# Gelu expert layer: GpSimd prepares the second spline expert's weights, and that expert's store and the fifth expert's load move ahead of the routed tiles

## The reference, cut to what matters

```python
hs = gelu(einsum('td,nfd->ntf', t, sw1) + sb1)           # 2 shared experts, F = 512
shared = einsum('ntf,ndf->td', hs, sw2) + sb2.sum(0)
probs = softmax(t @ gate_w.T + gate_b)                    # 8 routed experts
top_v, top_i = top_k(probs, 2)
hr = gelu(einsum('td,efd->etf', t, rw1) + rb1)
routed = einsum('etd,te->td', einsum('etf,edf->etd', hr, rw2) + rb2, cw)
out = shared + routed
```

```python
spline = einsum('nic,oic->no', b_splines(x), spline_w * scaler[..., None])   # three such layers per expert, 8 experts
```

## Time and profile before

| | us |
|---|---|
| median of 3 runs | 922.3 |
| the three runs | 946.85, 922.3, 920.98 |
| profiled execution | 915.97 |
| its span | 914.2 |
| TensorE busy | 787.8 |
| VectorE busy | 619.0 |
| ScalarE busy | 559.5 |
| GpSimd busy | 287.9 |

### The profile page before, as it was taken

One profiled execution on the slowest core, in us unless ns is written; L12 is line 12 of the kernel. 1 busy time (PEld: TensorE's weight loads), 2 busy tenths in 40 slices (PEclk: granted clock), 3 DMA queues, 4 the chain that ended last, 5 costly groups with the idle time before them and its releaser, 6 DMA issues.

```text
span 914.2 us, 21932 instructions
## 1 busy us (share of the span) xinstructions
PE 787.8 (86%) x7434; PEld 739.0 (81%) x7434; DVE 619.0 (68%) x1347; ACT 559.5 (61%) x1339; POOL 287.9 (31%) x320
## 2 busy tenths in 40 slices
PE   4987999688950896549999999999999999999992
PEld 3865699677640684449999999999999999999992
DVE  3898869262565496554777777777787777777752
ACT  4872537454400794234888877778777777787650
POOL 1770056240565384011132222332232222222111
PEclk9995999798985597558999999999999999999997
DMA  9602668998892000262357362244544334420000
GB/s 350 277 4 66 277 180 318 358 373 316 334 419 84 1 3 23 77 244 85 110 166 269 88 221 87 63 124 154 166 165 164 122 108 146 136 61 11 8 7 6
DMA packets 53603, 141.08 MB, mean 154 GB/s; under 512 B 6459, under 2 KB 29381, under 8 KB 46373
## 3 DMA queue, kind: packets, MB, share of 16 engines
q1 hardware_dynamic: 40996, 110.47, 33.0%
q10 hardware_dynamic: 3408, 20.06, 5.7%
q0 software_dynamic: 9136, 9.77, 5.6%
HBM read 106.65 MB, written 33.62 MB: 153 GB/s over the span
## 4 chain that ended last, share of the span: by engine, by line
PE 53%; DVE 3%; ACT 1%; DMA 1%; issue 1%; POOL 0%; DVEq 0%; POOLq 0%; ACTq 0%
PE kan_ps_h L1607 33%; PE kan_ps_y L1621 17%; DMA kan_slot_x<-normed_dram,slots 1%; PE kan_ps_slots L1288 1%; PE kan_ps_slots L1296 1%; PE kan_ps_lists L1274 1%; PE kan_ps_x L1595 0%; PE kan_ps_h L1270 0%; DMA out<-kan_y_sb,kan_slots_y 0%; ACT kan_xt L1654 0%; DVE kan_hf L1756 0%; DVE kan_hfar L1752 0%; DVE kan_hnear L1753 0%; ACT kan_hnear L1668 0%; DVE kan_hf L1760 0%
## 5 line engine op out<-in xcount | busy, mean ns | idle before, releaser
L1607 PE MATMUL kan_ps_h<-kan_xf,kan_w 128*128 128x128 f32 x2496 | 306.3, 276 | 0.0
L1607 PEld LDWEIGHTS kan_ps_h<-kan_xf,kan_w 128*128 128x128 f32 x2496 | 293.3, 193 | 0.0
L1621 PE MATMUL kan_ps_y<-kan_w,kan_hf 128*128 128x128 f32 x1248 | 154.2, 277 | 8.3 <-DVE kan_hf L1760 8.3
L1621 PEld LDWEIGHTS kan_ps_y<-kan_w,kan_hf 128*128 128x128 f32 x1248 | 147.5, 194 | 8.8 <-issue 8.8
L1837 POOL DMA_INDIRECT out<-kan_y_sb,kan_slots_y x39 | 63.5, 1628 | 240.3 <-ACT kan_y_sb L1705 240.3
L1752 DVE TENSOR_TENSOR kan_hfar<-kan_ht,kan_hfar 128x1024 f32<-128x1024 f32 x39 | 48.1, 1233 | 84.4 <-ACT kan_hnear L1668 84.4
L1654 ACT ACTIVATE kan_ht<-kan_hu,kan_biases 128x256 f32<-128x256 f32 x156 | 66.2, 496 | 13.6 <-DVE kan_hu L1779 13.6
L1009 POOL DMA_INDIRECT f_slot_x<-normed_dram,f_tokens x39 | 42.7, 1096 | 96.7 <-DVE f_rows L1136 52.9
L554 DVE TENSOR_TENSOR sw_raw<-sw_raw,sw_scal 128x512 f32<-128x512 f32 x56 | 34.6, 691 | 50.3 <-DMA sw_scal<-in_scalers 50.3
L974 ACT ACTIVATE f_slot_h<-f_ps_up,f_wr 128x128 f32<-128x128 f32 x156 | 44.7, 369 | 38.0 <-DMA f_wr<-in_experts 22.5
L1680 ACT ACTIVATE kan_xu<-kan_ps_x 128x128 f32<-128x128 f32 x39 | 10.7, 273 | 86.1 <-PE kan_ps_x L1595 86.1
(11 more groups left out here) (247 smaller groups left out, 1589.6 us busy)
## 6 DMA issues: line engine op xcount, KB each, us to landing
kan_w<-w_dram SPq DMA_DIRECT2D x16, 2048.0 KB, 7.6
kan_w<-w_dram SPq DMA_DIRECT2D x16, 1024.0 KB, 5.2
sw_raw<-in_experts SPq DMA_DIRECT2D x15, 1024.0 KB, 10.8
w_dram<-sw_raw SPq DMA_DIRECT2D x15, 1024.0 KB, 16.9
w_dram<-sw_raw ACTq DMA_DIRECT2D x9, 1024.0 KB, 6.2
sw_raw<-in_experts ACTq DMA_DIRECT2D x9, 1024.0 KB, 6.9
f_wr<-in_experts SPq DMA_DIRECT2D x20, 258.0 KB, 5.6
f_wr<-in_experts SPq DMA_DIRECT2D x20, 256.0 KB, 4.7
```

Of the source, the lines that this page charges most:

```text
L1607: mm = eng.matmul(ps_h[n % 2][:, m, :], w12[n % 2][:, at:at + P], rhs, start=(c == 0), stop=(c == BASES))
L1621: mm = eng.matmul(ps_y[n % 2][:, :], lhs, w3[n % 2][:, i * P:(i + 1) * P], start=(i == 0), stop=(i == CH1 * FEAT - 1))
```

## The change

Four edits in `gelu_experts`:

- GpSimd's list gets `prepare_in_pieces(eng, 1)` at its head, ahead of the gathers. VectorE's loop no longer has expert 1.
- SP's list gets the store of expert 1 and the load of expert 4 behind the load of expert 3, ahead of the wait for `lots_ok` and so of every fetch of routed weights.
- ScalarE's table STORE loses expert 1, and the stores of 2 and 3 move to earlier tiles.
- ScalarE's table LOAD loses expert 4, and the loads of 5 and 6 move to earlier tiles.

```diff
@@ -742,10 +742,8 @@
-        STORE = {6: (1, 0), 8: (1, 1), 10: (1, 2), 12: (2, 0), 14: (2, 1), 16: (2, 2),
-                 27: (3, 0), 29: (3, 1), 31: (3, 2)}
-        LOAD = {15: (4, 0), 17: (4, 1), 18: (4, 2), 19: (4, 3), 21: (5, 0), 23: (5, 1), 25: (5, 2), 26: (5, 3),
-                35: (6, 0), 36: (6, 1), 37: (6, 2), 38: (6, 3)}
+        STORE = {4: (2, 0), 6: (2, 1), 8: (2, 2), 11: (3, 0), 22: (3, 1), 24: (3, 2)}
+        LOAD = {14: (5, 0), 16: (5, 1), 18: (5, 2), 19: (5, 3), 30: (6, 0), 32: (6, 1), 34: (6, 2), 35: (6, 3)}
@@ -786,6 +784,8 @@
                 splines.store(eng, 0)
                 splines.load(eng, 3)
+                splines.store(eng, 1)
+                splines.load(eng, 4)
                 eng.wait_ge(lots_ok, 1)
@@ -1016,6 +1016,7 @@
+                splines.prepare_in_pieces(eng, 1)
                 eng.wait_ge(kept, 32)
                 eng.wait_ge(tokens_ok, 1)
@@ -1139,7 +1140,7 @@
-                for e in range(1, 4):
+                for e in range(2, 4):
                     splines.prepare_in_pieces(eng, e)
```

## The result

The changed kernel takes 951.84 us (median of 4 runs, 950.51 to 956.48), the kernel before 922.64 (median of 4). The ratio is 1.0349 with a 95% interval of 1.0304 to 1.0395: 3.5% slower, some 32 us. I had forecast 918 in a range of 907 to 929. The profiled execution's span is 948.7 us against 914.2, 34.5 us more.

The account below looks back on a forecast made before the run. The prediction took the gelu layer's routed tiles to be DMA-bound, with 24.0 us of TensorE waits. Its terms, 3.5 + 2.5 - 8.8 - 1 = -3.8 us, scaled to the median, gave 918 us, range 907 to 929.

Parts of the forecast that it names:

- What bounds the kernel: Gelu layer's routed tiles: DMA-bound from 160 to 225 us, TensorE losing 24.0 us in three groups of waits for weights.
- The model of the stalls: Routed tiles: bytes asked for at 2.7 us a megabyte, against the time the tiles need, give the loss by group.
- The 4.5 us that I carried along: Tiles 29 to 36 before the change: 7.8 us lost where bytes gave 3.3; the difference was added to the new forecast.
- GpSimd gains 18 instructions: Head of the gelu layer: 18.8 us of GpSimd work, done at 92.4, hidden by 27 us unless it disturbs VectorE.
- The lock: Rival: GpSimd's tensor_tensor and VectorE's two-SBUF-input instructions take turns in preparing expert 0; 5.2 us later, 924; chance 0.27.
- SP's store 1 and load 4: SP's queue ahead of the weight fetches: load 4 leaves at 117.7, the tiles start 3.5 us later (bounds 0 to 8).
- The clock after that wait: TensorE's first tiles: half clock after standing still 3.5 to 4 us ahead of tile 0, costing 2.5 us.
- Fewer bytes: Routed tile loop with the new tables: 15.2 us lost instead of 24.0, so 8.8 gained (bounds 7 to 14).
- ScalarE waits: Expert 2's first store piece at tile 4, 138.8: preparation done at 136.6, so no wait, by 2.2 us.
- The tail: Gather-backs behind the tiles: load 6 issued five tiles earlier shrinks the 6.23 us gather at 259.73; 1 us gained.
- The sum of the moved DMAs: Whole layer: late start 3.5 and clock 2.5, less 8.8 for bytes and 1 for the tail, makes -3.8 us.
- the stalls don't shrink: Rival: fetches queue behind whatever piece is in flight, so tiles still lose 24 us; +6 us, 928; chance 0.14.

Follow-up runs that it names:

- e5: Kernel before, with every spline-weight piece that ScalarE issues among the routed tiles cut to 8 columns: 906.33 us, ratio 0.9878.
- e7: Changed kernel without GpSimd's 18 preparation instructions (expert 1 unscaled) and with gaps in VectorE's preparations: 917.7 us, ratio 0.9997.
- e3: Changed kernel, with GpSimd waiting for the 16 normalisations before it prepares expert 1: 929.15 us, ratio 1.0148.
- e2: Changed kernel with GpSimd's 18 preparation instructions left out, only semaphores raised, the moved DMAs kept: 931.77 us, ratio 1.0137.
- e4: Changed kernel, with VectorE waiting for itself behind nearly each piece of its preparations (gaps): 933.37 us, ratio 1.0161.
- e10: Kernel before, with VectorE's preparations as five long instructions per expert instead of 18 short ones: 927.71 us, ratio 1.0097.
- e6: Kernel before, with VectorE waiting for itself behind nearly each piece of its preparations (gaps): 918.41 us, ratio 1.0008.
- e1: Kernel before, with only GpSimd preparing expert 1 in VectorE's place, SP's list and ScalarE's tables untouched: 939.87 us, ratio 1.0223.
- e8: Changed kernel, with GpSimd waiting for the normalisations and gaps in VectorE's preparations: 920.9 us, ratio 1.0027.
- e11: e8 with SP's load 4 moved behind the fetches of the first four tiles: 927.92 us, ratio 1.0083 to the kernel before.

## Why the prediction was wrong

**What bounds the kernel: right. The model of the stalls: right in the sum alone.** With 20 MB taken away the tiles lose 17.6 us fewer (e5), but 6.4 stay where the model left at most 4. By group the model was wrong. In e7 tiles 16 to 20 lost 6.1 us (forecast for 14 to 20: 5.9), tiles 20 to 28 lost 4.6 (0.5) and tiles 28 to 36 lost 5.1 (8.8). The sum of these three is 15.8 against 15.2. That is luck: 4.1 us too few in the middle group and 3.7 too many in the last cancel. The 4.5 us that I carried along in the last group without a reason did not come; 4.3, the figure by bytes alone, was nearer to the 5.1.

**GpSimd gains 18 instructions: this step failed.** I wrote "So it is hidden by 27 us, unless it disturbs VectorE (a rival, below)". Hidden it was as work of GpSimd's own. The disturbance, which the sum put at nothing, cost 15.8 us: it fell on the 16 short normalisations between 75.7 and 79.8, the first thing that the whole layer waits for. e3 shows it from the other side: with GpSimd behind them they take 4.19 us again.

**The lock, as a rival: the mechanism right, place and price wrong.** I counted GpSimd's first six instructions as done undisturbed while VectorE normalised, and charged only VectorE's five long instructions, 5.2 us. In the run the five long products and subtractions paid nothing, because GpSimd was done by then, and each of 16 short instructions paid one GpSimd instruction, 0.93 us more than its own 0.26. The price of taking turns is set by the number of instructions that meet, and I had looked for the longest ones. The Trainium skill, page "SBUF — State Buffer", section "Who interferes with whom", holds that tensor_scalar can enter a 2-port mode and then contends with GpSimd, as instructions with two SBUF inputs do; by both rules the forecast's chance for this rival, 0.27, was too low. The traces agree with it in every row above: tensor_scalar 1.19 us beside GpSimd where 0.26 is its own, steps with two SBUF inputs up to 1.25 where 0.29 is theirs, reductions and statistics unchanged. They do not show which mode tensor_scalar runs in.

**A gather held for 19.93 us: no step of the prediction had it.** I had the row of it in hand, the gather-back of 6.23 us at 259.73, took it for one place in the tail, and named it beside the lock without a price for gathers. It is the same thing: it ends at 265.96, 0.92 us after VectorE's preparation of expert 7 gave way to an instruction with one SBUF input:

```profile
265.04 1.48 DVE L1081 TENSOR_TENSOR x_sb<-x_sb,f_ps_dn 128x512 f32<-128x512 f32 x2
```

In the changed kernel the one at 292.95 ends at 298.34, 0.90 after 297.44. The one at 153.21 ends at 173.14, 0.82 after window_bias has ended at 172.32. There the next instruction starts at 172.35; back to back, each starts some 0.08 us before the end of the last, so the stream has a break of about 0.1 us. The held gather of e2 ends at the same place of the list, 0.81 us after window_bias. e4 shows that gaps end it (no run with gaps has a gather over 1.5 us) and e10 that a gather waits for VectorE's boundary. In pieces of 0.6 us the boundaries come often, and most gathers get in at the next one (0.94 to 1.49 us); the held ones missed boundary after boundary. Why they do, and what part of a gather it is that waits, is open.

**SP's store 1 and load 4: right in kind, too low.** Tile 0 was forecast 3.5 us late. It was 4.9 late in e7 and 7.0 in e2, where GpSimd prepares nothing and the held gather comes only later, and 6.9 in the changed kernel behind the normalisations. The 1.3 us for the first half to land stand in no row; in the kernel before the first eight halves landed 3.1 to 4.0 us after their issue. Load 4 went out at 119.98 in e2, 2.3 us later than I had it; 0.65 of them are the layer's later beginning (74.25 against 73.60).

**The clock after that wait: right.** Tile 0's 8 matmuls take 2.07 us in e7 as in the changed kernel, at the lower clock. In e7 tile 2 starts 5.5 us behind tile 0, before it was 3.5: 2.0 us of the 2.5 forecast.

**Fewer bytes: right in the net.** Forecast 8.8 us less lost and 2.5 us for the clock, 6.3 net; e7's tiles take 5.5 less, with the groups as above.

**ScalarE waits: not reached.** In the changed kernel expert 2 was prepared at 156.67, and its first store went out only at 176.89, behind the held gather.

**The tail: not confirmed.** e6 has no held gather and is the same.

The sum of the moved DMAs was forecast at -3.8 us; e7 measures a ratio of 0.9997, that is -0.3 with some 2 us either way. Over the chain of waits the 35.5 us at tile 38 read: 1.8 from before the layer, the normalisations 15.8, SP's chain 6.9, the tiles 11.0. Of the tiles' 11.0 the held gather makes 12.0 by e4 (107.2 us less 95.2), less 1.0 for the bytes; by e7's tiles (90.75) it would be 16.5, less 5.5. Single traces don't settle that split.

**The rival "the stalls don't shrink"** is refuted by e7: its tiles lose 18.6 us and not 24, and its time is not 6 us over. e5 doesn't speak against it, since it cuts the pieces themselves. The rival had the sign of the result by another mechanism.

## What to carry to other kernels

Before giving GpSimd elementwise work beside VectorE, list the VectorE instructions that it will meet: each with two SBUF inputs, and each fp32 tensor_scalar from SBUF to SBUF, may pay one whole GpSimd instruction (1.04 us here), so a run of short ones on the path is the worst neighbour, and a stretch of reductions or statistics the best. An indirect gather that GpSimd issues while VectorE streams two-input instructions can be held until the stream breaks; a wait of VectorE for itself behind nearly each instruction of the stream cost nothing that could be measured here (e6: 1.0008) and removed holds of up to 20 us. A row of an odd length in the trace of before (one gather of 6.2 us among many of 0.94) deserves an explanation before the change is priced, since the change may move it onto the path.

## What the runs showed that I had not expected

- GpSimd and VectorE pass SBUF to each other per instruction: 16 tensor_scalar of 0.26 us and 18 GpSimd instructions of 1.04 us interleave at 1.19 to 1.23 us a pair (changed kernel, e1, e4). The one with long instructions loses nothing: GpSimd's first 8 took 19.91 us instead of 8.3 beside VectorE's long products, which kept their own time (e3).
- An indirect gather takes 0.94 us alone and ends 0.90 to 0.92 us after the VectorE instruction has begun at whose start it gets in; with VectorE instructions of 4.4 and 2.3 us it takes 4.33 and 1.89 (e10).
- 20 MB fewer in the tile loop shortened the tiles by 17.6 us (e5). Moving 6.7 MB ahead of them took 5.5 us out of the tiles and gave 4.9 of it back as a later start (e7), and putting load 4, 3.5 MB, between the first fetches and the next cost 0.6% over e8 (e11).
